# Sums before maxima, a border instead of a whole clear, and small products between large ones, in a four-block image kernel

## The chip, the cores and the metric

The kernel runs on one core of one Trainium2 chip. The metric is the device time of one launch in microseconds (us). One launch works through 16 images of 192 channels and 32 x 32 pixels, one image after another.

## The reference, cut to what matters

Each image goes through four blocks. Each of them normalises the image in groups of six channels and adds its result to it.

```python
x = x + _L0_conv_ref(_gn(x), ...)   # attention, 6 heads
x = x + _L1_conv_ref(_gn(x), ...)   # selective scan in 4 directions, layer norm, gelu
x = x + _L2_conv_ref(_gn(x), ...)   # depthwise 3x3, the 30 highest scores of a channel kept
x = x + _L3_conv_ref(_gn(x), ...)   # the "mix", below
```

The scan's step sizes are `dt = softplus(dts + bias)`, and each direction reads `dt` and `dt * u` (`u` is the source). The part of the mix that matters here:

```python
zxbcdt = useq @ in_proj_w.T                   # z 384, xBC 448, dt 12 columns
z, xBC = ...
dt = softplus(zxbcdt[..., DI + CONV_DIM:] + dt_bias)
xBC = conv2d(xBC, kern, 'SAME', depthwise)    # 3x3, zero border
...
dA_cs = cumsum(dt * A)                        # over chunks of 128 tokens
```

## The kernel before, in words

The kernel is one loop over the images, with a barrier at its end. Each of the five engines has a program of its own in the loop, written out by hand, and the programs wait for each other on semaphores. Nothing is scheduled by a planner: an engine issues its instructions in the order in which the code writes them.

A pass of the loop has two parts. In the first part the scan of image b (96 steps) runs interleaved with the attention and the set-up of the scan for image b + 1. Its last piece is called the scan's tail here. In the second part only image b is at work: its convolution with the top 30, and its mix. What is late in the tail, the convolution or the mix is late for the whole pass.

**The tail.** ScalarE takes six logarithms, one for each unit of the next image's `dt` (`setup_act`). VectorE turns each into a finished `dt` with a maximum against its linear part (`setup_dve`, L640, 128 x 1024), and GpSimd multiplies it by the source (`setup_pool`, L648, 128 x 1024). SyncE writes `dt` and the product to DRAM (`setup_sp`), waits for all, and raises `f_out`. The image at hand needs VectorE's `taken(3)` (L1170), which takes the last sums of the scan from PSUM into `YA`. TensorE then works out means and, after VectorE's centring (L1203) and ScalarE's squares, variances (both L1038, 128 x 512 products in float32). Logarithm, exponential, VectorE's scaling (L1210), gelu and addition to the image (L1216) follow.

**A group norm** is five short steps. VectorE takes statistics of the image (L349, L358, L361), TensorE sums them over groups (`norm_pe`, L410), VectorE makes a shift and a variance of them (L373 to L379), GpSimd takes the root (`norm_pool`, L417), and VectorE writes the normalised image in four pieces, two for each half (L392). Norm 2 comes before the convolution, norm 3 before the mix. `keep_clock(n, at)` (L1005) issues n idle bfloat16 products of 512 columns on TensorE; 16 of them stand behind norm 3's sums.

**The convolution.** GpSimd clears the padded image (L1290) and makes nine diagonal weights (L1292). TensorE convolves the first 128 channels (L1278), and VectorE the other 64 and the top 30 of both (L1307 to L1326). The last of these raises `k_x` to 2.

**The mix** begins with GpSimd's clear of the padded image `CP` (L1844, 128 x 4624) and of two smaller tiles (L1845, L1846). TensorE projects the normalised image five times (`project(s)`, L1440, four products of 512 columns for each s). ScalarE copies projections 0 to 3 into `CP` (L1595). TensorE's `ps[2]` receives the 12 `dt` columns in 16 products (L1450: eight groups of 128 tokens, two channel parts each), which stand behind projection 2. In float32 each product is two records in the trace. VectorE convolves tile 0 (`convolve(0, range(9))`, L1684 and L1687), adds the `dt` bias (L1716) and clamps (L1719), convolves a part of tile 1, and, after ScalarE's exponential and logarithm, finishes `dt` (L1723) and its signed copies `dAR` (L1727, L1733). GpSimd convolves a part of tile 2 as soon as it is in (L1697, L1703). TensorE convolves five taps of tile 3 (L1457), then waits for `dAR` and sums `dt` up (L1471 to L1475). ScalarE takes the high parts of these sums (L1609), VectorE their rests (L1738), and the chunks follow.

Of the kernel before, what the change touches and what calls it, by code (L numbers as in the profile page):

```python
# [88 lines left out]
def build(nc, x, out, wqk, wv, wp, pb, xpw, dtw, dtb, alog, ds, lnw, lnb, cw, cb, wz, wx, wdt,  # L89
# [3 lines left out]
    with ctx:  # L93
# [298 lines left out]
                nc.vector.tensor_scalar(dst[:, rows, :], src[:, rows, :], g_t[0:n, t, 0:1], g_t[0:n, t, 2:3],  # L392
                                        ALU.add, ALU.mult).then_inc(g_xn, 1)

        def norm_dve(dve, u, writes, x_in=X, begun=False, room=None):

            norm_sums(dve, u, x_in, begun)
            norm_var(dve, u)
            norm_rstd(dve, u)
            if room is not None:  # L400
                dve.wait_ge(room, 1)
            for m in range(2):
                norm_writes(m, writes, x_in)
# [753 lines left out]
        def scan_dve(dve, b, front):  # L1157
            def taken(g):

                dve.wait_ge(m_y, GROUP_END[g] + 1)  # L1160
                c = g % 2
                n = CT[c]
                if g < 2:
                    dve.wait_ge(m_ya, 32)
                    nc.vector.scalar_tensor_tensor(YA[0:n, c, :], YA[0:n, c, :], v_dsum[0:n, c:c + 1], ps[3][0:n, :],
                                                   ALU.mult, ALU.add).then_inc(m_ev, 1)
                else:
                    dve.wait_ge(m_ev, g - 1)
                    y = YA[0:n, c, :].rearrange("p (h w) -> p h w", w=W)
                    nc.vector.tensor_tensor(y, y, ps[3][0:n, :].rearrange("p (w h) -> p h w", h=H),  # L1170
                                            ALU.add).then_inc(m_ev, 1)

            for i in range(NSTEP):
                _, k, _, _, _, f = STEPS[i]
                next(front)
                dve.wait_ge(m_bu, i + 1)
                dve.wait_ge(m_da, i + 1)
                o = slice(None, None, -1) if k >= 2 else slice(None)
                if from_psum(i):
                    nc.vector.tensor_tensor_scan(ps[2][:, o], ps[2][:, o], step[:, i % NBUF, o], 0.0,  # L1180
                                                 ALU.mult, ALU.add).then_inc(m_h, 1)
                    if k:
                        dve.wait_ge(m_cb[k], 32)
                    else:
                        dve.wait_ge(p_c, 32 * b + 32)
                    dve.wait_ge(m_h, i + 1)
                    nc.vector.tensor_tensor(step[:, i % NBUF, :], ps[2][:], Cb[2 * (k // 2) + f],  # L1187
                                            ALU.mult).then_inc(m_hcv, 1)
                else:
                    nc.vector.tensor_tensor_scan(step[:, i % NBUF, o], ps[2][:, o], step[:, i % NBUF, o], 0.0,  # L1190
                                                 ALU.mult, ALU.add).then_inc(m_h, 1)
                next(front)
                for g_ in range(3):
                    if i == GROUP_END[g_] + 2:
                        taken(g_)
            setup_dve(dve, range(0, 4))
            taken(3)

            halves = [slice(HALF * h, HALF * h + HALF) for h in range(2)]
            for h in range(2):  # L1200
                dve.wait_ge(m_mu, h + 1)
                for c, m in enumerate(CT):
                    nc.vector.tensor_tensor(YA[0:m, c, halves[h]], YA[0:m, c, halves[h]], ps[0][0:m, halves[h]],  # L1203
                                            ALU.subtract).then_inc(m_ce, 1)
            setup_dve(dve, range(4, 6))
            for h in range(2):
                dve.wait_ge(m_rs, h + 1)
                for c, m in enumerate(CT):
                    dve.wait_ge(m_sq, 2 * h + c + 1)
                    nc.vector.tensor_tensor(YA[0:m, c, halves[h]], YA[0:m, c, halves[h]], RSTD[0:m, halves[h]],  # L1210
                                            ALU.mult).then_inc(m_n, 1)
            dve.wait_ge(m_xr, 32)
            for h in range(2):
                for c, m in enumerate(CT):
                    dve.wait_ge(m_ge, 2 * h + c + 1)
                    nc.vector.tensor_tensor(X[0:m, c, halves[h]], X[0:m, c, halves[h]], YA[0:m, c, halves[h]],  # L1216
                                            ALU.add).then_inc(m_x, 1)
                if h == 0:
                    dve.wait_ge(m_x, 2)
                    norm_stats(0)  # L1220
# [209 lines left out]
        def mix_pe(pe):  # L1430
            def project(s):
# [5 lines left out]
                for h in range(2):  # L1437
                    pe.wait_ge(g_xn, 8 + 2 * (h + 1))
                    for c, m in enumerate(CT):
                        mm = nc.tensor.matmul(ps[p][0:n, half(h)], w[0:m, c, lo:lo + n],  # L1440
                                              XN[0:m, c, half(h)], start=(c == 0), stop=(c == 1))
                mm.then_inc(b_zp, 1)

            for s in range(5):
                project(s)
                if s == 2:

                    for j in range(NCH):
                        for c, m in enumerate(CT):
                            mm = nc.tensor.matmul(ps[2][:, NH * j:NH * j + NH], XN[0:m, c, tokens(j)],  # L1450
                                                  w_dt3[0:m, c, :], start=(c == 0), stop=(c == 1))
                    mm.then_inc(b_dp, 1)
            def conv_bc(taps):

                for h, tap in taps:
# [129 lines left out]

        def mix_act(act):
            act.wait_ge(f_out, 1)
            act.wait_ge(b_z, 2)

            def projected(s):  # L1590
                act.wait_ge(b_zp, s + 1)
# [113 lines left out]
        def mix_dve(dve):  # L1705
# [2 lines left out]

            dve.wait_ge(f_out, 1)
            dve.wait_ge(b_zc, 1)  # L1710
            convolve(0, range(9))

            dve.wait_ge(b_dp, 1)
            bias = v_dtb3[:].unsqueeze(1).to_broadcast([128, NCH, NH])
# [2 lines left out]
                                    ALU.add).then_inc(b_d1, 1)  # L1717
            dve.wait_ge(b_d1, 1)
            nc.vector.tensor_scalar(e3, dtT[:, :, :], SOFTPLUS_LINEAR, None, ALU.min).then_inc(b_d2, 1)  # L1719
            dve.wait_ge(b_zc, 3)  # L1720
            convolve(1, range(0, 4))
            dve.wait_ge(b_d3, 2)
# [3 lines left out]
            da3 = dAT.rearrange("p (c h) -> p c h", h=NH)  # L1726
            nc.vector.tensor_tensor(da3, dtT[:, :, :], na, ALU.mult).then_inc(b_da, 1)  # L1727
            dve.wait_ge(b_da, 1)
            dve.wait_ge(b_z, 3)
            for sign in range(2):  # L1730
                for p in range(3):
                    at = 32 * p + NH * sign
# [105 lines left out]
            finish(1)  # L1838
            added(1)

        def mix_pool(pool):
            pool.wait_ge(f_out, 1)
            pool.wait_ge(k_x, 2)
            pool.memset(CP[:, :, :], 0.0).then_inc(b_z, 1)  # L1844
            pool.memset(prev[0:32, 0, :], 0.0).then_inc(b_z, 1)  # L1845
            pool.memset(dAR[:, :, :], 0.0).then_inc(b_z, 1)  # L1846
            pool.wait_ge(b_zc, 4)
            convolve_pool(pool)
            pool.wait_ge(b_st, 2)
# [57 lines left out]
        with nc.Fori(0, n_batch) as b:  # L1907
            with nc.Block() as block:
# [8 lines left out]
                @block.tensor  # L1917
                def _(pe):
                    scan_pe(pe, front_pe(pe))
                    norm_pe(pe, 2)  # L1920
                    conv_pe(pe)
                    norm_pe(pe, 3)
                    keep_clock(16, bank(6))
                    mix_pe(pe)
# [8 lines left out]
                def _(dve):  # L1933
                    scan_dve(dve, b, front_dve(dve, b + 1))
                    dve.wait_ge(m_x, 4)
                    norm_dve(dve, 2, lambda t, n: XPv[0:n, t, 1:1 + H, 1:1 + W], begun=True, room=k_z)
                    conv_dve(dve)
                    dve.wait_ge(k_x, 2)

# [5 lines left out]
                def _(pool):  # L1945
                    scan_pool(pool, b, front_pool(pool))
                    setup_pool(pool, range(0, 2))
                    conv_pool(pool)
                    setup_pool(pool, range(2, 6))
                    norm_pool(pool, 2)  # L1950
                    norm_pool(pool, 3)
                    mix_pool(pool)

# [66 lines left out]
```

## Time and the profile before

| | us |
|---|---|
| median of 3 runs | 12510.87 |
| lowest and highest | 12497.52, 12556.97 |
| profiled execution, its own time | 12547.2 |
| its span | 12545.4 |

The profiled execution is 0.3% above the median. Its mean granted TensorE clock is 0.83 of full speed. Around the 16 passes of the loop stand the set-up and the first image's attention, some 500 us. The pass shown in the rows is the second one; its convolution ends at 1846.96 us and its mix at about 2016 us.

### The profile page before, as it was taken

The page shows a single profiled execution, that of the slowest core. Times are in us where ns is not written, and L with a number is a line of the kernel's source. Part 1 is how long each engine was busy: PE and PEld are TensorE (multiplying, and loading weights), DVE is VectorE, ACT ScalarE, POOL GpSimd, SP SyncE. Part 2 cuts the span into 40 slices and gives each one's busy share as a digit, 9 for nine tenths or more (in the row PEclk, how much of TensorE's full clock was granted, in tenths as well). Part 3 has the DMA queues.
Part 4 walks back from the last instruction along what each step waited for, and adds up shares of the span by engine and source line. Part 5 has one row for each costly group of instructions (what it writes and reads, how often), then busy time and mean ns, then how long its engine had stood idle before and what let it go on. Part 6 is the DMA issues. An engine that isn't in the chain of part 4 may idle for free. (4 is left out here: it accounts for less than half of the span.)

```text
span 12545.4 us, 91862 instructions
## 1 busy us (share of the span) xinstructions
PE 10024.8 (80%) x28440; PEld 2891.6 (23%) x28440; DVE 8217.2 (65%) x7943; ACT 4364.8 (35%) x5374; POOL 7729.8 (62%) x3710
## 2 busy tenths in 40 slices
PE   6787878878778787878878778787878878778787
PEld 1112122122222212122122222212222122222212
DVE  2367666666766666666666766667666666766666
ACT  1243333423334243333424334243333424334243
POOL 0384756838567483756838567483856848566583
PEclk9697888979788897878879788787878979788897
DMA  0352542524335152543524335252533524345252
GB/s 14 89 123 63 122 109 69 123 68 115 88 89 142 49 123 60 125 106 73 122 69 116 83 96 135 53 119 60 127 105 73 126 66 118 81 100 131 56 122 57
DMA packets 358663, 1181.05 MB, mean 94 GB/s; under 512 B 67483, under 2 KB 68747, under 8 KB 358023
## 3 DMA queue, kind: packets, MB, share of 16 engines
q1 hardware_dynamic: 331703, 1157.28, 37.0%
q10 hardware_dynamic: 24800, 15.62, 0.5%
q8 instruction: 259, 4.24, 0.1%
q14 instruction: 381, 3.12, 0.1%
q0 software_dynamic: 1520, 0.78, 0.1%
HBM read 1004.06 MB, written 156.02 MB: 92 GB/s over the span
## 5 line engine op out<-in xcount | busy, mean ns | idle before, releaser
L1235 POOL TENSOR_TENSOR arena<-arena 128x1024 f32<-128x1024 f32 x1536 | 3664.8, 2401 | 740.5 <-issue 718.1
L1251 POOL TENSOR_TENSOR arena<-arena 128x1024 f32<-128x1024 f32 x1152 | 2714.7, 2357 | 1358.3 <-DVE arena L1190 1355.7
L1016 PE MATMUL ps<-arena,sel_y 128*32 128x512 f32 x6144 | 3317.2, 675 | 200.1 <-POOL arena L1251 177.4
L1190 DVE TENSOR_TENSOR_SCAN arena<-ps,arena 128x1024 f32<-128x1024 f32 x1152 | 2628.1, 2281 | 659.1 <-ACT ps L1128 640.8
L1128 ACT ACTIVATE ps<-arena,v_na 128x1024 f32<-128x1024 f32 x1536 | 1716.6, 1118 | 3466.6 <-DVE arena L1190 2393.1
L917 DVE TENSOR_REDUCE arena<-ps 128x1 bf16<-128x512 f32 x1632 | 1113.1, 682 | 1321.6 <-PE ps L700 1321.6
L869 ACT ACTIVATE arena<-ps 128x512 f32<-128x512 f32 x1632 | 880.2, 591 | 846.9 <-PE ps L725 846.5
L1016 PEld LDWEIGHTS ps<-arena,sel_y 128*32 128x32 f32 x6144 | 602.9, 118 | 2405.1 <-issue 2016.6
L1180 DVE TENSOR_TENSOR_SCAN ps<-ps,arena 128x1024 f32<-128x1024 f32 x384 | 879.7, 2291 | 383.1 <-ACT ps L1128 324.4
L700 PE MATMUL ps<-arena 32*128 32x512 bf16 x1632 | 676.9, 415 | 474.0 <-DVE arena L917 474.0
L725 PE MATMUL ps<-arena 33*128 33x512 f32 x3264 | 994.0, 688 | 73.5 <-ACT arena L832 55.0
L737 PE MATMUL ps<-arena 128*64 128x512 f32 x3264 | 990.5, 688 | 0.0
L410 PE MATMUL ps<-g_mv,c_group 128*128 128x3 f32 (+1 forms) x528 | 130.2, 342 | 880.9 <-DVE g_mv L361 530.2
L417 POOL TENSOR_TENSOR g_t<-g_t,v_root 128x2 f32<-128x2 f32 x66 | 46.9, 711 | 972.9 <-DVE g_t L379 972.9
L700 PEld LDWEIGHTS ps<-arena 32*128 32x128 bf16 x1632 | 150.8, 92 | 1689.0 <-DVE arena L917 1019.8
L1187 DVE TENSOR_TENSOR arena<-ps,arena 128x1024 f32<-128x1024 f32 x384 | 470.4, 1225 | 45.8 <-DVE ps L1180 7.5
L1687 DVE SCALAR_TENSOR_TENSOR arena<-arena,v_mcw 128x1024 f32<-128x1024 f32 (+1 forms) x384 | 456.9, 1190 | 13.1
L1697 POOL TENSOR_SCALAR arena<-arena,v_mcw 128x640 f32<-128x640 f32 x144 | 164.2, 1143 | 468.2 <-ACT arena L1595 468.2
L1669 POOL TENSOR_TENSOR arena<-arena,c_heads 88x1536 bf16<-88x1536 bf16 x112 | 313.2, 2797 | 202.7 <-ACT arena L1624 199.5
L1859 POOL TENSOR_TENSOR arena<-arena 128x384 f32<-128x384 f32 x128 | 106.3, 831 | 484.5 <-DVE arena L1761 484.5
L725 PEld LDWEIGHTS ps<-arena 33*128 33x128 f32 x3264 | 259.7, 195 | 496.6 <-issue 305.9
L1595 ACT ACTIVATE arena<-ps 128x1024 f32<-128x1024 f32 x64 | 65.8, 1028 | 872.6 <-PE ps L1440 872.6
(217 smaller groups left out, 11915.7 us busy)
## 6 DMA issues: line engine op xcount, KB each, us to landing
arena<-scan_dtu SPq DMA_DIRECT2D x770, 512.0 KB, 6.1
arena<-scan_dt SPq DMA_DIRECT2D x770, 512.0 KB, 4.7
arena<-scan_bc SPq DMA_DIRECT2D x260, 512.0 KB, 6.7
scan_dt<-arena SPq DMA_DIRECT2D x68, 512.0 KB, 8.1
scan_dtu<-arena SPq DMA_DIRECT2D x68, 512.0 KB, 4.8
scan_dt<-arena SPq DMA_DIRECT2D x68, 256.0 KB, 4.1
scan_dtu<-arena SPq DMA_DIRECT2D x68, 256.0 KB, 4.8
XN<-arena SPq DMA_DIRECT2D x204, 64.0 KB, 4.2
```

The source lines that it names most:

```text
L700: nc.tensor.matmul(bank(3), QR[at:at + DH, t, Q * j:Q * j + Q], KR[at:at + DH, t, HALF * m:HALF * m + HALF], start=True, stop=True).then_i ...
L725: nc.tensor.matmul(bank(e), KK[r, t, Q * j:Q * j + Q], QQ[r, t, HALF * m:HALF * m + HALF], start=True, stop=True).then_inc(a_st, 1)
L737: mm = nc.tensor.matmul(bank(2)[64 * e:64 * e + 64, :], V[:, j, 2 * t + e, :], PT[:, 2 * (u % 2) + e, :], start=(j == 0), stop=(j == 7))
L869: nc.scalar.activation(PT[:, 2 * (u % 2) + e, :], bank(e), ACT.Exp, scale=DH ** -0.5).then_inc(a_e, 1)
L917: nc.vector.reduce_max(MXH[:, i // 2, i % 2:i % 2 + 1], bank(3), AX.X).then_inc(a_m, 1)
L1016: mm = nc.tensor.matmul(ps[3][32 * q:32 * q + 32, HALF * h:HALF * h + HALF], sel_y[:, r, :], step[:, i % NBUF, HALF * h:HALF * h + HALF], ...
L1128: nc.scalar.activation(ps[2][:], dtr[:, i // 2 % DTR, :], ACT.Exp, scale=v_na[:, at:at + 1]).then_inc(m_da, 1)
L1180: nc.vector.tensor_tensor_scan(ps[2][:, o], ps[2][:, o], step[:, i % NBUF, o], 0.0, ALU.mult, ALU.add).then_inc(m_h, 1)
L1187: nc.vector.tensor_tensor(step[:, i % NBUF, :], ps[2][:], Cb[2 * (k // 2) + f], ALU.mult).then_inc(m_hcv, 1)
L1190: nc.vector.tensor_tensor_scan(step[:, i % NBUF, o], ps[2][:, o], step[:, i % NBUF, o], 0.0, ALU.mult, ALU.add).then_inc(m_h, 1)
L1235: pool.tensor_tensor(step[:, i % NBUF, :], dur[:, i // 2 % DUR, :], Bb[2 * (k // 2) + f], ALU.mult).then_inc(m_bu, 1)
L1251: pool.tensor_tensor(step[:, i % NBUF, :], step[:, i % NBUF, :], Cb[2 * (k // 2) + f], ALU.mult).then_inc(m_hcp, 1)
```

## The change

Six edits, all inside the loop:

1. VectorE takes only the maximum of unit 0 ahead of `taken(3)`. Units 1 and 2 come behind it, units 3 and 4 behind the centring, and unit 5 inside norm 2, between its statistics and its waiting step (`meanwhile`).
2. GpSimd's product of unit 5 goes behind norm 2's root.
3. GpSimd clears only the four border lines of each tile of `CP`, in two small clears instead of one large, and does all clears of the mix ahead of norm 3's root, as soon as `k_x` is 2.
4. TensorE issues `keep_clock(8)` ahead of the sums of norm 2 and of norm 3.
5. The 16 little `dt` products go between the large ones of projections 1 and 2: one group of 128 tokens behind each large product.
6. VectorE stops the convolution of tile 0 after six taps for the `dt` bias and clamp, and takes its last three taps behind them.

```diff
-            setup_dve(dve, range(0, 4))
+            setup_dve(dve, range(0, 1))
             taken(3)
+            setup_dve(dve, range(1, 3))
...
-            setup_dve(dve, range(4, 6))
+            setup_dve(dve, range(3, 5))
...
             norm_sums(dve, u, x_in, begun)
+            if meanwhile is not None:
+                meanwhile()
...
-                mm.then_inc(b_zp, 1)
+                        if c == 1 and h == 1:
+                            mm.then_inc(b_zp, 1)
+                        if s in (1, 2):
+
+                            project_dt(4 * (s - 1) + 2 * h + c)
+
+            def project_dt(j):
+                for c, m in enumerate(CT):
+                    mm = nc.tensor.matmul(ps[2][:, NH * j:NH * j + NH], XN[0:m, c, tokens(j)],
+                                          w_dt3[0:m, c, :], start=(c == 0), stop=(c == 1))
+                if j == NCH - 1:
+                    mm.then_inc(b_dp, 1)
...
-            convolve(0, range(9))
+            convolve(0, range(6))
             dve.wait_ge(b_dp, 1)
...
+            convolve(0, range(6, 9))
             dve.wait_ge(b_zc, 3)
             convolve(1, range(0, 4))
...
+        def mix_clear(pool):
             pool.wait_ge(f_out, 1)
             pool.wait_ge(k_x, 2)
-            pool.memset(CP[:, :, :], 0.0).then_inc(b_z, 1)
+            pool.memset(CPv[:, :, 0:PAD:PAD - 1, :], 0.0).then_inc(b_z, 1)
+            pool.memset(CPv[:, :, 1:1 + H, 0:PAD:PAD - 1], 0.0).then_inc(b_z, 1)
...
                     scan_pe(pe, front_pe(pe))
+                    pe.wait_ge(m_x, 2)
+                    keep_clock(8, bank(6))
                     norm_pe(pe, 2)
                     conv_pe(pe)
+                    pe.wait_ge(k_x, 2)
+                    keep_clock(8, bank(6))
                     norm_pe(pe, 3)
                     keep_clock(16, bank(6))
...
-                    setup_pool(pool, range(2, 6))
+                    setup_pool(pool, range(2, 5))
                     norm_pool(pool, 2)
+                    setup_pool(pool, range(5, 6))
+                    mix_clear(pool)
                     norm_pool(pool, 3)
```

## Rows read from the trace of the kernel before

**Rows 1.** Head of the page: the span.

```profile
span 12545.4 us, 91862 instructions
```

**Rows 2.** Single lines over all passes: duration ns min/median/max, first and last start.

```profile
L1844 POOL MEMSET arena<- x16: 3951/3951/3951, 1101.4 to 12372.2; 128x4624 f32 x16
L648 POOL TENSOR_TENSOR arena<-arena,XI x51: 2330/2348/3317, 499.2 to 12309.8; 128x1024 f32<-128x1024 f32 x51
```

**Rows 3.** Chain that ended last, last pass: start us, us, what.

```profile
12295.49 16.11 PE ps L1038 x16
...
12372.32 5.56 DVE XN L392 x2
```

**Rows 4.** Timeline, second pass, scan's tail: start, us, instruction, idle before it.

```profile
1765.58 10.22 DVE L640 TENSOR_TENSOR arena<-arena 128x1024 f32<-128x1024 f32 x4 [1.08 <-ACT arena L634]
...
1768.17 6.54 POOL L648 TENSOR_TENSOR arena<-arena,XN 128x1024 f32<-128x1024 f32 x2 [1.16 <-DVE arena L640]
1768.38 0.59 PE L1016 MATMUL ps<-arena,sel_y 128*32 128x512 f32 x1
...
1776.98 16.10 PE L1038 MATMUL ps<-arena,c_mean 128*128 128x512 f32 x16 [8.01 <-DVE arena L1170]
...
1779.13 3.15 POOL L1292 TENSOR_SCALAR arena<-c_ident,v_cw 128x128 f32<-128x128 f32 x9
...
1788.05 5.56 POOL L648 TENSOR_TENSOR arena<-arena,XI 128x1024 f32<-128x1024 f32 x2 [1.16 <-DVE arena L640]
...
1795.77 2.49 DVE L1210 TENSOR_TENSOR arena<-arena 128x512 f32<-128x512 f32 x4 [6.66 <-ACT arena L1150]
...
1804.18 2.13 PE L410 MATMUL ps<-g_mv,c_group 128*128 128x3 f32 x8 [11.11 <-DVE g_mv L361]
```

**Rows 5.** Stretches, second pass: busy us of PE, PEld, DVE, ACT, POOL, clock, DMA.

```profile
1771.30:1815.70 44.40, 24.00 (x31) 8.53 (x32) 27.15 (x37) 10.45 (x14) 19.45 (x17) 0.50 0.82 239
...
1856.70:1871.85 15.15, 13.70 (x30) 3.51 (x29) 10.29 (x10) 2.05 (x2) 1.93 (x3) 1.00 0.00 0
1871.85:1873.70 1.85, 1.85 (x13) 1.73 (x12) 1.78 (x3) 1.03 (x1) 0.00 (x0) 1.00 0.00 0
1873.70:1879.07 5.37, 5.37 (x22) 5.04 (x22) 2.54 (x2) 0.00 (x0) 0.00 (x0) 0.50 0.00 0
1879.07:1895.10 16.03, 16.03 (x18) 4.00 (x17) 8.57 (x14) 4.16 (x5) 6.53 (x7) 0.50 0.00 1
```

**Rows 6.** Timeline, second pass, norm 2 and norm 3.

```profile
1807.97 1.91 DVE L392 TENSOR_SCALAR arena<-X,g_t 128x512 f32<-128x512 f32 x4 [0.81 <-POOL g_t L417]
...
1852.09 5.88 PE L1005 MATMUL ps<-c_identb,c_zero 128*32 128x512 bf16 x16
...
1853.71 3.95 POOL L1844 MEMSET arena<- 128x4624 f32 x1
1853.81 6.47 DVE L392 TENSOR_SCALAR XN<-X,g_t 128x512 f32<-128x512 f32 x4 [0.81 <-POOL g_t L417]
```

**Rows 7.** Timeline, second pass, start of the mix.

```profile
1859.41 12.51 PE L1440 MATMUL ps<-XN,w_x 128*128 128x512 f32 x24 [1.45 <-DVE XN L392]
...
1871.85 7.29 PE L1450 MATMUL ps<-w_dt,XN 128*128 128x12 f32 x32
...
1887.19 1.03 ACT L1595 ACTIVATE arena<-ps 128x1024 f32<-128x1024 f32 x1 [14.21 <-PE ps L1440]
...
1891.44 0.26 DVE L1723 TENSOR_TENSOR arena<-arena 128x96 f32<-128x96 f32 x1 [7.14 <-ACT arena L1605]
...
1903.82 3.71 PE L1471 MATMUL ps<-c_upper,arena 128*88 128x128 f32 x16
...
1908.62 1.22 DVE L1738 TENSOR_TENSOR arena<-ps,arena 88x1024 f32<-88x1024 f32 x1 [2.55 <-ACT arena L1609]
```

**Rows 8.** Groups by shape, VectorE's taps, 1865 to 1877, then 1889 to 1907.

```profile
L1687 DVE SCALAR_TENSOR_TENSOR arena<-arena,v_mcw 128x1024 f32<-128x1024 f32 x8 | 10.3, 1285 | 0.3
...
L1687 DVE SCALAR_TENSOR_TENSOR arena<-arena,v_mcw 128x1024 f32<-128x1024 f32 x5 | 9.5, 1895 | 0.1
```

More of the change, by code:

```diff
@@ L393, in norm_writes, with norm_dve @@
                                         ALU.add, ALU.mult).then_inc(g_xn, 1)
-        def norm_dve(dve, u, writes, x_in=X, begun=False, room=None):
+        def norm_dve(dve, u, writes, x_in=X, begun=False, room=None, meanwhile=None):
             norm_sums(dve, u, x_in, begun)
+            if meanwhile is not None:
+                meanwhile()
             norm_var(dve, u)
@@ L1441, in project @@
                                               XN[0:m, c, half(h)], start=(c == 0), stop=(c == 1))
-                mm.then_inc(b_zp, 1)
+                        if c == 1 and h == 1:
[8 more added lines that the diff above has]
+                    mm.then_inc(b_dp, 1)
             for s in range(5):
                 project(s)
[L1446 to L1452, printed above, removed]
             def conv_bc(taps):
@@ L1587, in mix_act @@
             act.wait_ge(f_out, 1)
-            act.wait_ge(b_z, 2)
+            act.wait_ge(b_z, 3)
             def projected(s):
@@ L1728, in mix_dve @@
             dve.wait_ge(b_da, 1)
-            dve.wait_ge(b_z, 3)
+            dve.wait_ge(b_z, 4)
             for sign in range(2):
@@ L1839, in mix_dve, with mix_pool @@
             added(1)
-        def mix_pool(pool):
+        def mix_clear(pool):
             pool.wait_ge(f_out, 1)
             pool.wait_ge(k_x, 2)
-            pool.memset(CP[:, :, :], 0.0).then_inc(b_z, 1)
+            pool.memset(CPv[:, :, 0:PAD:PAD - 1, :], 0.0).then_inc(b_z, 1)
+            pool.memset(CPv[:, :, 1:1 + H, 0:PAD:PAD - 1], 0.0).then_inc(b_z, 1)
             pool.memset(prev[0:32, 0, :], 0.0).then_inc(b_z, 1)
             pool.memset(dAR[:, :, :], 0.0).then_inc(b_z, 1)
+        def mix_pool(pool):
             pool.wait_ge(b_zc, 4)
@@ L1935, in _ @@
                     dve.wait_ge(m_x, 4)
-                    norm_dve(dve, 2, lambda t, n: XPv[0:n, t, 1:1 + H, 1:1 + W], begun=True, room=k_z)
+                    norm_dve(dve, 2, lambda t, n: XPv[0:n, t, 1:1 + H, 1:1 + W], begun=True, room=k_z,
+                             meanwhile=lambda: setup_dve(dve, range(5, 6)))
                     conv_dve(dve)
```

## The prediction

> **What bounds the kernel now.** I read the page's head first [rows 1], then single lines over all passes [rows 2]. GpSimd's large clear runs 16 times, first at 1101.4 and last at 12372.2 us, so a pass lasts (12372.2 - 1101.4) / 15 = 751.4 us. All edits lie in the last 250 us of a pass. There only one image is at work and no engine is busy throughout, so the order of waits counts, not an engine's share. The chain of waits shows that the edited pieces are on it [rows 3]: the means and variances behind `taken(3)` take 16.11 us of it, and two pieces of norm 3's write 5.56 us. The timeline of one pass [rows 4, 6, 7] gives the waits, the stretches [rows 5] the granted clock, and the groups [rows 8] what a VectorE tap costs alone and beside GpSimd. Positions below are those of the second pass.
>
> **Part 1: the scan's tail (edit 1).** The last sum ends at 1768.38 + 0.59 = 1769.0 [rows 4]. Before, VectorE was in four maxima until 1775.8, so `taken(3)` ended at 1776.9 and TensorE began at 1776.98. Now one maximum stands ahead. It starts at 1765.58 as before and takes at most the mean of 2.55 us, so it is over by 1768.1. `taken(3)` (1.2 us) then ends at 1770.2, and the means start at 1770.25, 6.7 us earlier.
>
> The second gain is the clock. TensorE sat idle for 8.01 us ahead of L1038, and from 1771.3 to 1815.7 the granted clock was 0.50 (1.2 GHz) [rows 5]. The 16 records took 16.10 us, 1.01 us each. With 1.2 us of idle time in place of 8 I expect 1.00 (2.4 GHz) to hold. The price at that clock is that of L1440, the same 128 x 512 float32 form, 12.51 / 24 = 0.52 us a record [rows 7]. The means then end at 1774.4. The maxima of units 1 and 2 sit ahead of the centring in VectorE's queue and end at 1772.7, so they delay it by 0.3 us at most. Squares follow, and the variances run from 1774.7 to 1778.9. Logarithm, table load and exponential as before put the first of the four L1210 at 1781.6 instead of 1795.77, a gain of 14.2 us.
>
> Now what is late next. GpSimd still owes the products of units 1 to 4. Alone such a product takes 2.35 us [rows 2]. Where both engines work on SBUF tiles they stretch each other: two products took 6.54 us, 3.27 each, while four maxima took 10.22 us, 2.55 each, against 1.2 for a lone one of this size [rows 4]. The differences, 0.9 and 1.3 us, are what is left of the other engine's instruction. So I model the two as taking turns, each waiting for the whole of the other's instruction. Counting GpSimd from 1768.17: product 0 to 1770.5, product 1 to 1775.0, the clear of 2.0 us, nine diagonals (3.15 us) to 1780.2, or 1781.2 if they meet the maximum of unit 4. Products 2, 3 and 4 then fall from 1780.3 to about 1789, just where the four L1210 stand. Before, GpSimd had finished at 1788.05 + 5.56 = 1793.6, ahead of 1795.77. By turns, the L1210 end at 1783.4, 1786.3, 1789.3 and 1789.9 instead of 1784.1; gelu keeps up. From the end of the L1210 to norm 2's sums VectorE needed 5.9 us (1798.3 to 1804.2), 0.2 of it a wait for gelu that falls away. Norm 2's sums start at 1795.5 to 1796.3 instead of 1804.18: a gain of 7.9 to 8.7, and I take 8.3. The bounds are 14.2, if the engines don't meet, and 6.0, if one more whole product of 2.35 us stands in the way.
>
> A rule of the Trainium skill says the same by another road: "SBUF — State Buffer", section "Who interferes with whom", gives VectorE and GpSimd one shared pair of ports under an exclusive lock, taken by a VectorE instruction with two SBUF inputs against a GpSimd one that reads SBUF, and by `tensor_scalar` in its fast mode against any GpSimd instruction. By that rule the products meet the L1210 as above and unit 5's meets the next step too; without it the sum would be 8.2 us a pass better.
>
> **Part 2: norm 2 (edits 1, 2, 4).** VectorE's maximum of unit 5 (1.2 us) falls into its wait for TensorE's L410 (2.13 us) and costs nothing while that is as long. `keep_clock(8)` begins at `m_x` 2, about 4.4 us ahead of the sums. At 1.2 GHz 8 such products take 3.4 us (the slow ones of 16 in 5.88 us stand 0.43 apart [rows 6]), so TensorE is free in time; a faster L410 would give 0.6 at most, and the maximum would take half of it. Nothing else waits there: TensorE's convolution is done well before ScalarE's copy of it is wanted. But GpSimd's product of unit 5 now stands directly behind the root, while VectorE starts L392 in the same moment. Beside the large clear, the same L392 took 6.47 us instead of 1.91 [rows 6]: the first piece waited for the whole clear. So I charge 2.3 us, a whole product; nothing, if VectorE comes first.
>
> SyncE's stores of the products now wait for unit 5, and `f_out` comes some 5 to 10 us later, near 1810. Its first reader is GpSimd's clear, some 30 us later, and the loads behind it serve the next pass, over 150 us away.
>
> **Part 3: norm 3 (edits 3, 4).** The clear held L392 for 5.56 us where two pieces alone take 0.96 [rows 3, 6]. Now GpSimd clears 272, 256, 384 and 704 elements, about 1.8 us at the clear's 0.85 ns an element, beneath the 2.46 us of statistics. That is worth 4.6 us to VectorE. TensorE gives most of it back. `keep_clock(8)` starts at `k_x` 2 (1847.0) and takes 3.4 us, 0.4 beyond the moment at which the sums are ready; L410 ends at 1852.55. The 16 idle products behind it took 5.88 us here (and 0.7 more, if the clock comes up later), so TensorE is free at 1858.4 to 1859.2, instead of starting the projections at 1859.41. The normalised half is there at 1855.2. So TensorE's own queue becomes the bound, and 4.6 shrinks to 0.3 to 1.0. If the eight idle products bring the clock up early, the 16 take 3.4 us and L410 is shorter, a gain of up to 4.1. I take 1.0.
>
> **Part 4: start of the mix (edits 5, 6).** Let T be the start of the projections (1859.41). TensorE ran at 1.00 until T + 14; the clock fell among the 32 records of L1450, and projections 3 and 4 went through at 0.50 (16.03 us for 16 records, against 8.3 at full) [rows 5, 7]. Interleaved, each large product brings TensorE back to work after four little records, and I expect 2.4 GHz to hold. At that level 12 weight loads of L1450 took 1.85 us, so 32 take 5.0 [rows 5]. Projections 0 to 2 and the little ones end at T + 12.4 + 5.1 = T + 17.5 (before T + 19.7), projection 3 at T + 21.7 (T + 27.7), projection 4 at T + 25.8 (T + 35.7), five taps of tile 3 at T + 30.1 (T + 44.4).
>
> VectorE now sets the end. Six taps end at T + 12.9. It waits until T + 17.6, bias and clamp take 0.5, the three other taps of tile 0 3.9, and four of tile 1 start at T + 22.1. GpSimd's convolution starts at T + 22.9 instead of T + 28.9, so the last three taps of these meet it, at 1.9 to 2.05 us instead of 1.29 [rows 8]. L1723 starts at T + 28.2; ScalarE has been ready since T + 26 (its copy at T + 21.8 plus the 4.25 us from L1595 to L1723 [rows 7]). Before, it was T + 32.0. `dAR` takes 5.1 as before, to T + 33.3, and TensorE now waits for it, where it was late at T + 44.4. The five taps left take 1.9 each, to T + 43.0, and L1738, which stood at T + 49.2 [rows 7], follows at once. That is 6.2 earlier; as the clock's rise in the cumulative sums (L1471) is not the same in all passes, I count 5.5. GpSimd's convolution still runs for some 6 us, 2 longer than before relative to L1738, and meets what VectorE does next: 1 us. I take 4.5, between 3.0 and 6.0. The rest of TensorE's taps ends near T + 50, ahead of its reader.
>
> **The sum.** 8.3 - 2.3 + 1.0 + 4.5 = 11.5 us a pass, 184 us for 16. The profiled execution would go from 12547 to 12363. It stands 36 us above the median of 12511, which would become 12327 us. Bounds: 7.0 a pass (6.0 - 2.3 + 0.3 + 3.0) gives 12399, and 24.3 (14.2 + 4.1 + 6.0, with no charge for unit 5) gives 12122.
>
> **The rivals.**
> - *The two engines do not meet.* Then the L1210 and L392 run as now, and a pass gains 14.2 + 1.0 + 4.5 - 2.3 = 17.4, or 278 us: 12233. For it: GpSimd's times move with its waits. Against it: the 6.54 and 6.47 us rows. Chance 0.13.
> - *The clock falls among the interleaved products.* Against: at 1.00 the first six little products went by before the level changed, and here only two stand between large ones. For: 1.00 was seen to hold only while large products came without a break [rows 5]. Fallen from the first little one on, projections 1 and 2 take 16.0, the little ones 8.5, projections 3 and 4 16.0. L1723 goes to T + 41 and the end of the five taps to T + 53.5: 9 us later than before instead of 4.5 earlier. A pass loses 8.3 - 2.3 + 0.3 - 9 = -2.7, and the time is 12554; a later fall gives 12450 to 12550. Chance 0.12. In "TensorE: Matmul & The Clock Gate", section "A second HAM failure mode: psum-queue depth-cycling", the Trainium skill says that short idle moments between groups of products can make the clock swing; by that rule this rival would be the likely one.
> - *The clock holds in neither place.* The means stay at 1.2 GHz too. Part 1 then gains only its earlier start, 6.3, as GpSimd is done by the time of L1210. A pass comes to 6.3 - 2.3 + 0.3 - 9 = -4.7, and the kernel is slower: 12586. It decides from the point where part 4 loses more than parts 1 to 3 gain, 4.3 us. Chance 0.06.
>
> **How the numbers follow.** My forecast has 0.69. What a measurement can tell from no change is about 0.5%, 63 us, so faster means below 12448. Forecast and first rival lie there: 0.82. The second rival is mostly within 0.5%: 0.12. The third and the worst of the second are slower: 0.06. The range reaches over the first rival and into the second: 12220 to 12470.
>
> **What would show each step.** L1038 should start 1.3 us behind the last sum, take 8.4 us at 1.00, and be followed by stretched L1210 (over 1.5 us each for two or three of them) beside L648. L392 of norm 2 should take 4.2 us, that of norm 3 1.9. TensorE's first L1440 should follow directly on its idle products, not on L392. The projections should show 1.00 throughout, and L1723 should follow a tap, not ScalarE. I would be wrong if the granted clock in the interleaved stretch is 0.50, or if L1210 stays at 0.68 us.

## The result, and the profile after

| | before | changed |
|---|---|---|
| median, us | 12533.92 (4 runs) | 12312.27 (4 runs) |
| lowest and highest | 12497.52, 12561.12 | 12291.14, 12341.96 |
| ratio, 95% interval | | 0.9825 (0.9803 to 0.9846) |
| profiled execution: own time, span, mean clock | 12547.2, 12545.4, 0.83 | 12291.14, 12289.3, 0.855 |

The change takes 222 us off, 13.9 us a pass; 11.5 were forecast. The lines of the changed kernel have moved by two to eight numbers: L1213 is L1210 of before, L1443 is L1440, L1453 is L1450, L1464 is L1457, L1478 is L1471, L1731 is L1723 and L1746 is L1738. Its L1723, in the rows below, is the bias step that was L1716. The table names steps by the lines of before.

```profile
span 12289.3 us, 92390 instructions
```

**Where a pass became shorter.** Each row is a stretch between two marks in the trace, as the mean over the 16 passes of the profile (15 for the last row). The marks are the end of the last scan sum, the start of norm 2's sums (L410), the end of norm 2's write, the end of the convolution, T (start of the projections), the start of L1738, the start of the first chunk (the first transpose, L1484), and what is called the end of the mix here: the end of VectorE's last step ahead of the last output products (L1791). The mix's last addition to the image ends 7.9 us later before the change and 7.6 after it, so the last row holds this piece too. Between the end of norm 2's write and the end of the convolution both take 37.09.

| stretch, us | before | changed | gain | forecast |
|---|---|---|---|---|
| last sum to norm 2's sums | 35.22 | 27.03 | 8.2 | 8.3 |
| norm 2's sums to end of its write | 5.70 | 7.25 | -1.55 | -2.3 |
| end of convolution to T | 12.45 | 8.25 | 4.2 | 1.0 |
| T to L1738 | 48.60 | 42.67 | 5.9 | 5.5 |
| L1738 to first chunk | 15.27 | 19.13 | -3.9 | -1.0 |
| first chunk to end of mix | 91.97 | 91.98 | 0.0 | 0 |
| end of mix to the next last sum | 505.05 | 501.41 | 3.6 | 0 |

The tail, the convolution and the mix together give 12.9 a pass. The last row is code that nobody touched; experiment e5 looks at it.

**The scan's tail**, timeline of the second pass of the changed kernel (start, us, instruction, what ended the idle time before it); it answers to [rows 4].

```profile
1756.49 0.59 PE L1018 MATMUL ps<-arena,sel_y 128*32 128x512 f32 x1
...
1757.12 1.21 DVE L1172 TENSOR_TENSOR arena<-arena,ps 64x1024 f32<-64x1024 f32 x1 [0.91 <-PE ps L1018]
...
1758.39 8.66 PE L1040 MATMUL ps<-arena,c_mean 128*128 128x512 f32 x16 [1.31 <-DVE arena L1172]
...
1769.25 2.35 POOL L650 TENSOR_TENSOR arena<-arena,XN 128x1024 f32<-128x1024 f32 x1
1769.75 8.79 DVE L1213 TENSOR_TENSOR arena<-arena 128x512 f32<-128x512 f32 x4 [3.49 <-ACT arena L1152]
...
1771.55 4.64 POOL L650 TENSOR_TENSOR arena<-arena,XI 128x1024 f32<-128x1024 f32 x2
```

`taken(3)` now waits for the last sum and not for maxima. The means and variances start 1.31 us behind it and take 8.66 us instead of 16.10. Then the four L1213 stand beside three products of GpSimd and take 8.79 us instead of 2.49. How they share the time is in the single line of L1213, over all passes (duration ns min/median/max):

```profile
L1213 DVE TENSOR_TENSOR arena<-arena x64: 673/675/6986, 1034.0 to 12063.7; 128x512 f32<-128x512 f32 x32, 64x512 f32<-64x512 f32 x32
```

One of them takes up to 7.0 us and the middle one 0.68. In this pass the products run from 1769.25 to 1776.2 and the four L1213 end at 1778.54. So I read it that the first waits until all three products are through, and the other three run at their own speed. The forecast had them take turns. The sum comes out alike (8.8 against 8.3), the way is another.

**Norm 2 and norm 3**, same pass and view; it answers to [rows 6].

```profile
1787.85 2.34 POOL L650 TENSOR_TENSOR arena<-arena,XI 128x1024 f32<-128x1024 f32 x1
1787.91 3.92 DVE L392 TENSOR_SCALAR arena<-X,g_t 128x512 f32<-128x512 f32 x4 [0.81 <-POOL g_t L419]
```

```profile
1828.98 3.60 PE L1007 MATMUL ps<-c_identb,c_zero 128*32 128x512 bf16 x8 [19.85 <-DVE X L1329]
1829.05 0.33 POOL L1854 MEMSET arena<- 128x272 f32 x1 [38.87 <-DVE X L1329]
...
1832.51 1.32 PE L412 MATMUL ps<-g_mv,c_group 128*128 128x3 f32 x8
1833.76 3.63 PE L1007 MATMUL ps<-c_identb,c_zero 128*32 128x512 bf16 x16
...
1835.48 1.91 DVE L392 TENSOR_SCALAR XN<-X,g_t 128x512 f32<-128x512 f32 x4 [0.81 <-POOL g_t L419]
1837.32 1.12 PE L1443 MATMUL ps<-XN,w_x 128*128 128x512 f32 x2
```

Unit 5's product costs norm 2's write 2.0 us. In norm 3 the write is back at 1.91. The eight idle products brought the clock up: the sums take 1.32 us instead of 2.1, the 16 idle products 3.63 instead of 5.88. In all 16 passes T lies between 8.1 and 8.4 us behind the convolution's end, and the projections follow directly on the idle products; the first normalised half was there 0.8 us earlier.

**The mix**, second pass and then the first one.

```profile
1854.39 0.26 DVE L1723 TENSOR_TENSOR arena<-ps,v_dtb 128x96 f32<-128x96 f32 x1 [4.18 <-PE ps L1453]
...
1864.11 1.59 DVE L1731 TENSOR_TENSOR arena<-arena 128x96 f32<-128x96 f32 x1
...
1870.58 3.39 PE L1478 MATMUL ps<-c_upper,arena 128*88 128x128 f32 x16 [3.35 <-DVE arena L1741]
...
1874.32 11.37 PE L1464 MATMUL ps<-arena,diag 64*64 64x512 f32 x26
...
1879.98 1.21 DVE L1746 TENSOR_TENSOR arena<-ps,arena 88x1024 f32<-88x1024 f32 x1
...
1896.91 0.90 PE L1491 MATMUL ps<-c_ident,arena 128*128 128x128 f32 x3 [3.93 <-ACT arena L1628]
```

```profile
1138.12 22.45 PE L1464 MATMUL ps<-arena,diag 64*64 64x512 f32 x26
...
1163.94 0.90 PE L1491 MATMUL ps<-c_ident,arena 128*128 128x128 f32 x3 [0.69 <-ACT arena L1628]
```

Stretches of the same passes (busy us of the five engines, clock, DMA), the interleaved products first:

```profile
1841.70:1854.30 12.60, 12.60 (x49) 6.54 (x48) 7.18 (x6) 2.60 (x3) 0.00 (x0) 1.00 0.00 1
...
1867.20:1870.60 3.40, 0.04 (x2) 0.02 (x1) 3.40 (x7) 0.00 (x0) 3.32 (x4) 0.92 0.00 0
1870.60:1874.30 3.70, 3.70 (x20) 3.62 (x20) 3.63 (x3) 0.29 (x1) 3.62 (x2) 0.61 0.00 0
1874.30:1885.70 11.40, 11.39 (x27) 3.36 (x26) 10.37 (x8) 5.15 (x5) 11.15 (x8) 1.00 0.00 0
```

```profile
1137.50:1161.00 23.50, 23.50 (x32) 6.44 (x32) 19.92 (x20) 6.92 (x7) 13.42 (x9) 0.50 0.00 0
```

The clock stays at 1.00 (2.4 GHz) all through the interleaved products. It falls behind them, while TensorE waits 3.35 us for `dAR`. In the second pass it comes back at once, tile 3's last 26 records take 11.37 us, and the chunks start at T + 59.6. In the first pass the level is 0.50 (1.2 GHz), the same records take 22.45 us, and ScalarE and the chunks wait for them: T + 63.5. Nine of the 16 passes are like the first. They are just those in which T lies 8.1 to 8.2 us behind the convolution; in the seven others it lies 8.4 behind, as the clock rose later in norm 3. So whether the level comes back behind the wait goes together with when it rose before the projections. Why, no run here shows.

### The profile page after: what moved, and what is told of

Same layout as the page of the kernel before. It is cut to its first block and busy times, and to the rows that moved or that the text cites. A ratio compares the mean times of both kernels' runs of the same rounds, so it can differ in the third digit from the quotient of the medians.

```text
span 12289.3 us, 92390 instructions
## 1 busy us (share of the span) xinstructions
PE 9828.4 (80%) x28696; PEld 2832.1 (23%) x28696; DVE 8246.4 (67%) x7943; ACT 4365.1 (36%) x5374; POOL 7719.5 (63%) x3726
## 5 line engine op out<-in xcount | busy, mean ns | idle before, releaser
L1007 PE MATMUL ps<-c_identb,c_zero 128*32 128x512 bf16 x816 | 242.0, 456 | 522.6 <-DVE X L1329 305.0
L1704 POOL TENSOR_SCALAR arena<-arena,v_mcw 128x640 f32<-128x640 f32 x144 | 207.3, 1442 | 388.6 <-ACT arena L1602 388.6
```

## The experiments

Times are medians of five runs unless said otherwise, ratios are to the kernel before.

**e1: nine taps ahead of the wait.**

```diff
-        AHEAD = 5
+        AHEAD = 9
```

> Changed kernel with AHEAD = 9 in place of 5: nine taps of tile 3 stand ahead of TensorE's wait for dAR, 18 records instead of 10. Theory A (the clock falls in the 3.35 us wait for dAR, and in 9 of 16 passes the other taps then run at 1.2 GHz): the wait disappears, the cumulative sums start 0.2 us later, the chunks start at T + 59.6 in every pass instead of T + 63.4 in nine, which is 2.1 us a pass and 34 us in all, about 12280 us. Theory B (the fall has another cause, a phase of the clock that the wait does not set): nine passes stay late and the time stays near 12312 us.

Measured: 12268.42 us, ratio 0.9803 (0.9781 to 0.9824). The second pass, TensorE:

```profile
1860.81 7.94 PE L1464 MATMUL ps<-arena,diag 64*64 64x512 f32 x18
1868.68 1.98 PE L1478 MATMUL ps<-c_upper,arena 128*88 128x128 f32 x16
...
1871.01 7.94 PE L1464 MATMUL ps<-arena,diag 64*64 64x512 f32 x18
```

The wait is gone, the cumulative sums take 1.98 us instead of 3.39, and from L1738 to the first chunk it is 16.91 us in each of the 16 passes (19.13 on average without). That is 2.2 us a pass, 35 us; the medians differ by 44. The interval overlaps that of the changed kernel (0.9803 to 0.9846), so the times alone would not settle it; the stretches do. Theory A holds.

**e2: without the eight idle products.** Both `keep_clock(8)` and their waits are out.

```diff
-                    pe.wait_ge(m_x, 2)
-                    keep_clock(8, bank(6))
                     norm_pe(pe, 2)
...
-                    pe.wait_ge(k_x, 2)
-                    keep_clock(8, bank(6))
                     norm_pe(pe, 3)
```

> Changed kernel without the two keep_clock(8). Theory A (they bring the clock up ahead of the sums, so that the 16 idle products behind take 3.45 us instead of 5.9 to 6.6): the projections start 11.1 to 11.7 us after the convolution's end instead of 8.25, and norm 2's sums take 2.1 us instead of 1.3; 3.9 us a pass, about 12375 us. Theory B (as predicted: they bring no clock, and the small clears alone give what norm 3 gained): the projections start at 8.3 or earlier and the time stays within 12 us of 12312.

Measured: 12366.85 us, ratio 0.9863 (0.9841 to 0.9885). Norm 3, second pass:

```profile
1838.51 2.14 PE L412 MATMUL ps<-g_mv,c_group 128*128 128x3 f32 x8 [21.89 <-DVE g_mv L361]
1840.58 5.50 PE L1007 MATMUL ps<-c_identb,c_zero 128*32 128x512 bf16 x16
...
1842.31 1.91 DVE L392 TENSOR_SCALAR XN<-X,g_t 128x512 f32<-128x512 f32 x4 [0.82 <-POOL g_t L419]
1846.01 4.29 PE L1443 MATMUL ps<-XN,w_x 128*128 128x512 f32 x8
```

VectorE is done at 1844.2, TensorE's own idle products end at 1846.0. Its queue is the bound, as the forecast described, with the eight or without; without them it ends later, as the 16 take 5.50 us and not 3.63. T is 10.88 us behind the convolution instead of 8.25. The two `keep_clock(8)` are worth 55 us. Theory A holds.

**e3: the little products in one block again.**

```diff
-                        if s in (1, 2):
-
-                            project_dt(4 * (s - 1) + 2 * h + c)
...
             for s in range(5):
                 project(s)
+                if s == 2:
+                    for j in range(NCH):
+                        project_dt(j)
```

> Changed kernel with the 16 little dt products in one block behind projection 2 again; VectorE's order stays changed. Theory A (the block lets the clock fall): projections 3 and 4 at 1.2 GHz, L1723's counterpart at T + 32, the rest of dAR's and the cumulative sums' times at T + 44, chunks at T + 63.9 instead of T + 61.8 on average: 2.1 us a pass, about 12346 us. Theory B (the gain of this part came from VectorE's new order and GpSimd's earlier start alone): chunks within 0.5 us of the changed kernel's, about 12312 us.

Measured: 12329.31 us, ratio 0.9849 (0.9829 to 0.9869). TensorE, second pass:

```profile
1851.30 6.41 PE L1450 MATMUL ps<-w_dt,XN 128*128 128x12 f32 x32
1857.63 8.08 PE L1443 MATMUL ps<-XN,w_x 128*128 128x512 f32 x8
```

Projection 3 needs 8.08 us instead of 4.29, and T to L1738 goes from 42.67 to 47.96. The first chunk comes only 1.5 us a pass later (63.31 against 61.80 from T), since the changed kernel loses at tile 3 what this one does not. That is 24 us; the medians differ by 17. Theory A holds in its mechanism. Its size, 34 us, is at the edge of what the runs can tell from 17: this kernel's interval overlaps that of the changed one.

**e4: GpSimd's products in the top 30.**

```diff
-                    setup_pool(pool, range(2, 5))
                     norm_pool(pool, 2)
-                    setup_pool(pool, range(5, 6))
+                    pool.wait_ge(k_m, 10)
+                    setup_pool(pool, range(2, 6))
```

> Changed kernel with GpSimd's products of units 2 to 5 moved behind norm 2's root and behind VectorE's first maximum of the top 30 (a wait on that step's semaphore). Theory A (VectorE and GpSimd take turns where both read SBUF tiles, so that the products stretch L1210 from 2.5 to 8.8 us and norm 2's write from 1.9 to 3.9): both go back to 2.5 and 1.9, norm 2 starts about 5.8 us earlier, and a pass takes 7.8 us less: about 12187 us. Theory B (the products cost VectorE the same wherever they stand, up to 4 x 2.3 us in the top 30): the top 30 grows by 5 to 9 us and the time stays near 12312. Theory C (f_out, now behind them, comes later than the end of the convolution): the clears and the mix wait for it, and the projections start later than 8.3 us after the convolution.

Measured: 12240.02 us, ratio 0.9775 (0.9756 to 0.9794).

```profile
L1213 DVE TENSOR_TENSOR arena<-arena x64: 674/677/693, 1034.6 to 12022.0; 128x512 f32<-128x512 f32 x32, 64x512 f32<-64x512 f32 x32
```

No L1213 takes over 0.69 us now, and norm 2's write is back at 1.91. The last sum is 21.08 us ahead of norm 2's sums instead of 27.03, norm 2 takes 5.29 instead of 7.25: 7.9 us, as theory A had it. The convolution with its top 30 takes 37.14 instead of 37.09, so the products cost nothing there (not B), and the clears start on time (not C). But the medians differ by 72 us, not by 125. The trace shows where the rest went. Tile 3's taps are slow in 13 passes instead of nine (1.0 us a pass), five passes start the projections at over 10 us because the clock came up later (0.9 us a pass on average), and the chunks take 93.55 us instead of 91.98. With these the stretches give 4.5 us a pass, 71 us. A stretch that starts earlier meets other levels of the clock.

**e5: the kernel before, once more** (one run, 12494.4 us).

> The kernel before, unchanged, profiled once more. It tells how much of the 3.6 us a pass by which the scan's own part (from the end of one mix to the last sum of the next scan, whose code nobody edited) was shorter in the changed kernel's profile is chance. Theory A (chance of the clock's level): its mean moves by 1 to 3 us from 505.1. Theory B (a lasting effect of the change): 505 again, against 501 to 503.5 in the five changed kernels profiled.

From the end of the mix to the next last sum this profile of the same program has 501.61 us instead of 505.05, and its span is 12492.6. Single passes lie between 495 and 509 us in both. Theory A holds: two profiles of one program differ here by as much as the last row above shows. It is the first profile of before that was long. Of all 14 profiles of this case it has the highest mean; the others lie between 501.4 and 503.9.

**e6: edits 1 and 2 alone**, on the kernel before (their lines of the diff above, with GpSimd's unit 5 behind norm 2's root).

> The kernel before with edits 1 and 2 alone (maxima behind the last sums, unit 5 inside norm 2). Theory A (the parts add): from the last sum to norm 2's sums 27.0 us instead of 35.2, norm 2's write 2.0 us longer for unit 5's product, nothing else in the tail moves: 6.2 us a pass, 99 us, about 12425 us. Theory B (the earlier finish is given back in norm 2, as SyncE's stores and f_out come later): under 3 us a pass, above 12480 us.

Measured: 12443.89 us (6 runs), ratio 0.9934 (0.9912 to 0.9956), 5.2 us a pass from the ratio. From the last sum to norm 2's sums 27.03, norm 2 7.71 instead of 5.70: 6.2 us, as theory A had it. From T to the first chunk it is 0.5 us less, and the chunks are 1.8 us longer than before (93.81 against 91.97), which brings the 6.2 down to 4.9. The expected 12425 us left this out.

**e7: the clock without the earlier start**, on the kernel before.

```diff
-            keep_clock(5, bank(3))
+            keep_clock(41, bank(3))
```

> The kernel before with keep_clock(41) in place of keep_clock(5) ahead of the means: 7.8 us more of idle products on TensorE, while it waits for taken(3), which keeps its old place behind four maxima. It parts the clock from the earlier start. Theory A (the idle wait let the clock fall): the 16 records of the means and variances take 8.6 us instead of 16.1; L1210 comes 7 us earlier and meets the product of unit 5, which costs 0 to 2.3: 5 to 7.5 us a pass, 12407 to 12445 us. Theory B (the records are slow for another reason, the stores to DRAM that run at the same time, DMA share 0.5 to 1.0): 16 us as before, and the time stays near 12525.

Measured: 12497.96 us (12 runs), ratio 0.9975 (0.9962 to 0.9988). Second pass, then L1210 over all:

```profile
1768.73 7.72 PE L1005 MATMUL ps<-c_identb,c_zero 128*32 128x512 bf16 x35
...
1776.09 1.20 DVE L1170 TENSOR_TENSOR arena<-arena,ps 64x1024 f32<-64x1024 f32 x1
1777.35 8.50 PE L1038 MATMUL ps<-arena,c_mean 128*128 128x512 f32 x16 [0.90 <-DVE arena L1170]
```

```profile
L1210 DVE TENSOR_TENSOR arena<-arena x64: 673/2274/2824, 1043.4 to 12253.9; 128x512 f32<-128x512 f32 x32, 64x512 f32<-64x512 f32 x32
```

The idle products keep the clock up, and the 16 records take 8.50 us at the old place, with the same stores to DRAM beside them. So the clock alone explains their price (not B): the DMA share beside them is 0.69 here and 0.64 before, the granted clock 1.00 and 0.50. But my size for A was wrong: of the 6.7 us by which L1210 comes earlier, 2.8 reach norm 2's sums. The four L1210 take 6.8 us, as two of them wait for a product each. A faster TensorE ran into GpSimd's queue. And as in e6 the chunks are longer than before, 93.83 us against 91.97, while T to the first chunk is 0.8 shorter. That leaves 1.7 us a pass, and 0.25% in the medians.

**e8: e1 and e4 together.**

> The changed kernel with both: GpSimd's products of units 2 to 5 in the top 30, and AHEAD = 9. Theory A (what the late products gave back stands in tile 3's taps and other places where the clock falls): from L1738's line to the chunks 16.9 us in every pass instead of 20.1; 3.2 us a pass less than with the late products alone, about 12190 us. Theory B (the two do not add, because the give-back is in the scan): about 12220 us or more.

Measured: 12177.73 us, ratio 0.9722 (0.9697 to 0.9747). 16.91 us from L1738 to the chunks in every pass and chunks back at 91.97: theory A. T stays late in some passes: 9.51 us behind the convolution on average instead of 8.25.

**e9: the one large clear again**, behind norm 3's root.

```diff
-            pool.memset(CPv[:, :, 0:PAD:PAD - 1, :], 0.0).then_inc(b_z, 1)
-            pool.memset(CPv[:, :, 1:1 + H, 0:PAD:PAD - 1], 0.0).then_inc(b_z, 1)
+            pool.memset(CP[:, :, :], 0.0).then_inc(b_z, 2)
...
-                    mix_clear(pool)
                     norm_pool(pool, 3)
+                    mix_clear(pool)
```

> The changed kernel with edit 3 undone: one clear of the whole padded image again, and all clears of the mix behind norm 3's root. Theory A (the clear held VectorE's write, and keep_clock(8) alone brings little here): TensorE is done with its idle products at 8.3 us behind the convolution, the first half is written at about 11.9, so the projections start 3.6 us later: 58 us, about 12370 us; and the idle time of 3.6 us may let the clock fall before the projections, which would cost up to 17 us a pass more. Theory B (TensorE's own queue is the bound, as the prediction had it): the projections start where they do in the changed kernel, 12312 us.

Measured: 12593.99 us, ratio 1.0055 (1.0041 to 1.0070): slower than the kernel before. Second pass:

```profile
1851.51 3.95 POOL L1854 MEMSET arena<- 128x4624 f32 x1
1851.60 6.47 DVE L392 TENSOR_SCALAR XN<-X,g_t 128x512 f32<-128x512 f32 x4 [0.81 <-POOL g_t L419]
...
1857.21 8.70 PE L1443 MATMUL ps<-XN,w_x 128*128 128x512 f32 x10 [3.70 <-DVE XN L392]
```

```profile
1857.20:1890.00 32.80, 32.79 (x59) 13.93 (x60) 10.64 (x12) 3.09 (x3) 0.00 (x0) 0.52 0.00 0
1890.00:1911.00 21.00, 21.00 (x24) 5.10 (x22) 17.38 (x18) 5.19 (x6) 14.11 (x11) 0.50 0.00 0
```

The clear costs its 3.8 us (T at 12.01 instead of 8.25). TensorE has then been idle for 3.70 us. The level is still 1.00 when the projections begin, falls to 1.2 GHz 1.3 to 1.7 us behind their start in all 16 passes, and the interleaved products do not bring it back: T to L1738 takes 59.50 us instead of 42.67. From L1738 to the first chunk 4.0 us come back (15.10 instead of 19.13), so the first chunk is 12.8 us later. Over the whole pass the stretches lose 17.8 us; the medians differ by 282 us, 17.6 a pass. This is the forecast's second rival seen at work. Its price there was 13.5 us (9 and 4.5) up to the chunks, against 12.8 here. The edit undoes both halves of edit 3, the size of the clear and its place, and does not tell them apart.

**e10: nine taps of tile 0 ahead of the bias** (edit 6 undone).

```diff
-            convolve(0, range(6))
+            convolve(0, range(9))
...
-            convolve(0, range(6, 9))
```

> The changed kernel with edit 6 undone: VectorE takes all nine taps of tile 0 ahead of the dt bias. Theory A (with the products interleaved the nine taps end just as the dt products do, T + 17; the split only pushes three taps into the stretch beside GpSimd's): L1723's counterpart waits for ScalarE and starts at T + 26.1 instead of T + 26.8, L1738's counterpart at T + 41.3 to T + 42 instead of T + 42.7; 0.7 to 1.4 us a pass, 12290 to 12301 us. Theory B (the split gives the exponential an earlier start): L1723 starts later than T + 26.8 and the time is above 12320 us.

Measured: 12262.06 us, ratio 0.9783 (0.9766 to 0.9799), so edit 6 costs 50 us. Second pass (T at 1833.4):

```profile
1850.46 0.26 DVE L1723 TENSOR_TENSOR arena<-ps,v_dtb 128x96 f32<-128x96 f32 x1 [0.22 <-PE ps L1453]
...
1858.93 0.26 DVE L1730 TENSOR_TENSOR arena<-arena 128x96 f32<-128x96 f32 x1 [3.33 <-ACT arena L1612]
```

```profile
1864.06 1.98 PE L1478 MATMUL ps<-c_upper,arena 128*88 128x128 f32 x16 [0.78 <-DVE arena L1740]
```

The nine taps end 0.2 us ahead of the `dt` products. VectorE then idles 3.33 us for ScalarE and still comes to L1738 2.6 us earlier (40.09 against 42.67 from T), for it has no taps beside GpSimd's first ones: the maximum of `dt` starts 1.3 us earlier and takes 0.26 us instead of 1.59. `dAR` is ready earlier, TensorE waits 0.78 us for it and not 3.35, and tile 3's taps are fast in all passes. That second gain I had not expected. The chunks give 1.2 us back (93.20 against 91.98). In five passes they take 91.4 us, in eleven 94.0 to 94.2, and in these the granted clock is 0.91 from 40 to 60 us behind the first chunk, where it is 1.00 in the five.

**e11: idle products in the waits behind tile 3**, on e8's kernel: `keep_clock(38, bank(3))` behind the last tap and `keep_clock(20, bank(3))` behind the first exponents.

> The fastest kernel so far (late products, AHEAD = 9) with 38 idle products of TensorE behind the last tap of tile 3 and 20 behind the first exponents, into the free half of ps[1], while it waits for VectorE. Theory A (the clock falls in these two waits of some 9 and 5 us, and the first chunks run at 1.2 GHz): the part from the chunks' start to the mix's end goes from 92.0 to 90.5 us or less, about 12155 us. Theory B (the chunks are bound by VectorE and ScalarE, and TensorE's level does not matter there): 92.0 stays, about 12178 us.

Measured: 12169.52 us, ratio 0.9716 (0.9702 to 0.9731). From the first chunk to the end 91.82 instead of 91.97: theory B. In the first 10 us of the chunks the granted clock is 0.66 to 0.71 instead of 0.50, and passes of the same kind take the same time as in e8: 91.6 us where T lies 8.2 us behind the convolution, 92.5 where it lies 8.6, and 91.5 where it lies 10.8. The 0.15 us is the mix of these kinds. So TensorE's level is not what bounds the start of the chunks. Further on a lower level goes with longer chunks (e10).

**e12: late products and nine taps.** e4's and e10's edits in one kernel.

> The changed kernel with the products of units 2 to 5 in the top 30 and all nine taps of tile 0 ahead of the dt bias; AHEAD stays 5. Theory A (the two gains stand in different stretches and add): from the last sum to norm 2's sums 21.1 us, from the projections to L1738's counterpart 40.1, from there to the chunks 16.9 in every pass; against the fastest kernel so far 2.6 us a pass less, 41 us, about 12137 us, at most 12160 if the clock gives some of it back in the chunks. Theory B (they do not add): 12178 us or more.

Measured: 12144.62 us (12135.41 to 12161.19), ratio 0.9706 (0.9691 to 0.9721). The stretches are 21.08, 40.09 and 16.92, the chunks 93.54. Theory A holds. It is the fastest kernel of the case, 168 us below the changed one, and this is more than e4's 72 and e10's 50: tile 3's taps, slow in 13 passes of e4, are fast in all passes here. The chunks keep what they took back in e4, and T is 9.42 us behind the convolution.

## Why the prediction was right, step by step

Right: 12327 was forecast, 12312 measured, within the range, and by mostly the right terms. That the two are 15 us apart is luck in part: 184 us off were forecast and 222 came, and the kernel before now stands at 12534, 23 above the 12511 from which the forecast counted.

- **Part 1, right in size.** 8.2 us against 8.3. The clock held, the records took 8.66 us against 8.4, the four L1210 ended where I had them. e7 shows the clock's part by itself, and e4 that the products take 6.0 us off the 14.2. Wrong in detail: they do not take turns; one L1210 waits for all three. The sign that I gave, two or three L1210 of over 1.5 us, did not show: one took 6.99 and the others 0.68. The end comes out alike, since either way the last product has to be through.
- **Part 2, right.** The write grew by 2.0 (2.3 forecast). L410 gave some back in nine passes, where the clock was up.
- **Part 3, the mis-sized term.** "TensorE gives most of it back", 1.0 a pass. It measured 4.2. The bound was right: in all 16 passes the projections follow on TensorE's own idle products, as the prediction's sign had it. The step that failed is that the eight idle products bring no clock: they did in all 16 passes, which I had only as the bound of 4.1. e2 shows T at 10.88 us once they are out, not far from the 11.45 of my 1.0.
- **Part 4, right up to L1738, wrong behind it.** T + 42.7 against T + 43.0. "The rest of TensorE's taps ends near T + 50, ahead of its reader" failed in nine of 16 passes, where it ended at T + 60. I had seen the new wait for `dAR` and not priced what it does to the clock. Over all passes part 4 gave 2.1 instead of 4.5. e1 and e10 remove the wait and the loss.
- **Edit 6** I took as part of the gain. e10 shows that it costs 50 us.
- **The sum.** 8.2 - 1.55 + 4.2 + 2.1 is 12.9 a pass against 11.5: too low by 3.2 in part 3, too high by 2.4 in part 4. That these two misses nearly cancel is luck. The runs' 13.9 differs by 1 us a pass, within what chance moves the scan's own part (e5).
- **The rivals.** The engines do meet (L1213, e4). The first rival's sum was wrong by itself: it has L392 run as before and still takes off 2.3 for unit 5. Without that it is 19.7 us a pass and 12196 us. The clock held among the interleaved products, which followed there directly on idle products; e9 shows that 3.70 us of waiting ahead of them were enough to lose it, and that edits 3, 4 and 5 depend on each other. The rule of the Trainium skill that the prediction named for this rival ("TensorE: Matmul & The Clock Gate", section "A second HAM failure mode: psum-queue depth-cycling") did not describe the interleaved stretch, where the level stayed at 1.00.

## What to carry to other kernels

When a wait goes, look at what each engine's queue holds at the new time, not at the old: in the tail three products of another engine took 6 us of 14 (e4), and a faster clock alone was worth 0.25% (e7). Look behind the stretch too: in e6, e7, e10 and e12 the chunks, which no edit touched, took 1.2 to 1.9 us more. Price an idle wait on TensorE by what runs behind it: 3.35 us of waiting made the next 11 us of products take 22 in nine passes, and filling it with taps that had to be done anyway was free (e1). Edits that each help only as long as the clock is up should be measured together and one by one, since one of six can cost 50 us (e10), and one left out can turn the rest into a loss (e9).

## What the runs showed of the hardware

- VectorE's instruction on two SBUF tiles lasted as long as three GpSimd products in a row (one of 0.68 us took up to 6.99), while in the tail before the times fit turns (maxima of 1.2 us took 2.55 each, products of 2.35 took 3.27).
- Among 16 passes of one program the same 26 records took 11.37 or 22.45 us (changed kernel), and the untouched scan 495 to 509 us (before).
- A stretch of interleaved float32 products directly behind idle bfloat16 products stayed at 2.4 GHz (12.6 us at 1.00). Behind 3.70 us without work the level fell to 1.2 GHz within 2 us of its start and did not come back in the stretch (32.8 us at 0.52, e9).
- Four GpSimd products of 2.35 us beside VectorE's top 30 cost 0.05 us in 37 (e4); beside the four L1210 three of them cost 6 us.
